# Two DMA issues of the first attention moved: batch 0's value loads and the first store of maxima

## The chip, the cores and the metric

The kernel runs on one core of a Trainium2 chip. The metric is the time on the device, in microseconds. TensorE (PE), VectorE (DVE), ScalarE (ACT) and GpSimd (POOL) compute; SyncE (SP) only issues DMAs, and POOL issues some too. All DMAs of the core are carried by its 16 DMA engines.

## What is computed

Two transformer-like layers on x of shape 4 x 1024 x 128 in float32. The change lies in the first attention: 16 heads of width 8, a plain softmax over 1024 keys.

```python
def _L0_attn_ref(z, ln_scale, ln_bias, w_qkv, w_proj, b_proj):
    ...
    qkv = zn @ w_qkv
    ...
    scores = jnp.einsum('bhqd,bhkd->bhqk', q, k) / SCALING
    att = jax.nn.softmax(scores, axis=-1)
    out = jnp.einsum('bhal,bhlv->bhav', att, v)
    ...
    return z + out
x = L0_attn_z
xn = _layernorm(x, axis=-1)
s = _L0_attn_ref(xn, L0_attn_ln_scale, L0_attn_ln_bias, L0_attn_w_qkv, L0_attn_w_proj, L0_attn_b_proj)
g = _silu(_L0_ffn_ref(xn, ...))
x = x + s * g
```

The second layer (landmark attention and a mixture of experts) follows and isn't touched.

## The kernel before

The first attention is the function `layer0_attention`. Its unit is a pair of heads, `d`, of which there are 32 (`DUOS`); two pairs make a quad, whose operands lie in one of three slots (`SLOTS`). A quad's operands `b_q`, `b_k`, `b_qo`, `b_ko` and `b_v` come from DRAM with `load_quad`, which issues 13 DMAs on SP (four for each of three parts, and one for the values). Batch 0 is quads 0 to 3, pairs 0 to 7.

A pair is done in 8 groups `kb` of 128 keys (`TB` = 8). In each group PE makes four blocks of 512 scores (L724), ACT takes their exponential (L669), and PE multiplies the exponentials of the group before by the values (L700); `b_av` counts these finished groups over the whole stage, and so stands at 8 x d when pair d begins to be counted. Between groups PE makes the plain scores from which the row maxima of a pair further on are taken (L555, L556) and DVE reduces them (L611). In group 5 of pair d-1 PE transposes the maxima of pair d. DVE and POOL split the negated maxima into three bfloat16 parts `b_neg`, and SP stores them with three small DMAs into three more rows of that quad's `b_q` (`store_maxima`, L797 for each DMA). The matmuls L724 of pair d read these rows: PE waits for `b_m_loaded` before the first of them.

SP's order is written by hand: loads of quads 1 and 2, the maxima of pair 0, and then for each pair d the maxima of pair d+1, the numerators and sums of pair d (`store_values`, L804, four DMAs), in some pairs a piece of zeroing, and a part of a later quad (eight DMAs in odd steps, five in even ones). In the step d = 13 it is the eight.

Batch 0 is finished inside this stage (`EARLY` = 1). POOL loads its softmax sums, DVE inverts them, POOL stores the reciprocals, and in its step d = 14 POOL loads the numerators and the reciprocals (`load_values`, L761 into `d_num` and L763 into `d_den`, 512 KB each). DVE multiplies the two only at the end of pair 15 (L636), and PE projects the result in the last pair. POOL's step d begins with the maxima of pair d, that is in group 5 of pair d-1.

The prologue of the stage, before pair 0 can begin, is the maxima of pairs 0 and part of 1: PE and DVE alternate there, while quads 1 and 2 are being loaded.

Of the kernel before, what the change touches and what calls it, by code (L numbers as in the profile page):

```python
# [15 lines left out]
TB = T // P  # L16
# [148 lines left out]
SLOTS = 3  # L165
# [5 lines left out]
T_GROUP = 5  # L171
LEAD = ITEMS + LATE - 2 * T_GROUP
EARLY = 1
RECS = B - 1
PROJECT_AT = (0, 1, 2, 3)
E_RING = 12
# [346 lines left out]
def wait_for_parts(g, sp, b):  # L523

    for i in range(NPART):
        sp.wait_ge(g.sem(f"a_stored{i}"), STORED[i] * (b + 1))
    sp.wait_ge(g.sem("a_v_stored"), 16 * (b + 1))


def load_quad(g, sp, quad, c, parts=range(NPART + 1)):  # L530

    def moved(dst, src):
        sp.dma_start(dst, src).then_inc(g.sem(f"b_loaded{c}"), 16)

    for m in parts:
        if m == NPART:
            moved(g.v0[c][:, 0:HQ * P], g.v_ops[quad, :, :, :].rearrange("p h n -> p (h n)"))
            continue
        lo = NPART * HD * ((m + 2) % NPART)
        n = min(NPART * HD, MROWS - lo) // HD  # L540
        flat = "h i d t -> (i d) h t"
        moved(g.q0[c][lo:lo + NPART * HD, :, :], g.q_ops[quad, :, :, :, :].rearrange(flat))
        moved(g.k0[c][lo:lo + NPART * HD, :, :], g.k_ops[quad, :, m:m + NPART, :, :].rearrange(flat))
        odd = slice(MROWS + lo, MROWS + lo + n * HD)
        moved(g.qo[c][odd, :, :], g.q_ops[quad, 1:HQ:2, 0:n, :, :].rearrange(flat))
        moved(g.ko[c][odd, :, :], g.k_ops[quad, 1:HQ:2, m:m + n, :, :].rearrange(flat))
# [23 lines left out]
def layer0_attention(g):  # L570
# [6 lines left out]
    nc, sem = g.nc, g.sem  # L577
    with ExitStack() as mem:
# [6 lines left out]
        zeros = sb("b_zeros", [P, 2048])  # L585
        dens = sb("d_dens", [P, RECS, P])
        num = sb("d_num", [P, T])
        den = sb("d_den", [P, T])
        oT = sb("d_oT", [P, EARLY, T])
        sm = sb("d_small", [P, 5, TB])  # L590
# [11 lines left out]
    with nc.Block() as block:  # L602

        @block.vector
        def _(dve):
# [21 lines left out]
            for d in range(DUOS):  # L627
                for n in range(upto(d, -1), upto(d, TB - 1)):
                    item(n)
                b = d // 8 - 1  # L630
                if 0 <= b < RECS and d % 8 == 3:
                    dve.wait_ge(sem("d_dens"), 16 * (b + 1))
                    nc.vector.reciprocal(dens[:, b, :], dens[:, b, :]).then_inc(sem("d_recs"), 1)
                if 0 <= b < EARLY and d % 8 == 7:
                    dve.wait_ge(sem("d_loaded"), 32 * (b + 1))
                    nc.vector.tensor_tensor(oT[:, b, :], num[:, :], den[:, :], ALU.mult).then_inc(sem("d_oT"), 1)  # L636
            link = Link(dve, sem("d_step"))
            for b in range(EARLY):
                mine = slice(b * TB, (b + 1) * TB)
# [93 lines left out]
        @block.gpsimd  # L733
        def _(pool):
            nc.gpsimd.memset(zeros[:, :], 0.0).then_inc(sem("b_zeros"), 1)

            def parts(d):
                pool.wait_ge(sem("b_max_done"), seq.index((d, None)) + 1)
                nc.gpsimd.tensor_copy(neg[:, 1, :], neg_rest[:, :]).then_inc(sem("b_second"), 1)  # L739
                pool.wait_ge(sem("b_second"), d + 1)  # L740
                nc.gpsimd.tensor_tensor(neg[:, 2, :], neg_rest[:, :], neg[:, 1, :], ALU.subtract)\
                      .then_inc(sem("b_third"), 1)

            def load_sums(b):
                for s in range(2):
                    pool.wait_ge(sem(f"b_stored{s}"), 16 * 4 * 4 * (b + 1))
                src = g.av_out[b * 4:b * 4 + 4, :, HD, :].rearrange("q h (c t) -> (q h) c t", t=P)
                pool.dma_start(dens[:, b, :], src).then_inc(sem("d_dens"), 16)

            def store_reciprocals(b):  # L750
                pool.wait_ge(sem("d_recs"), b + 1)
                pool.dma_start(g.recs[b, :, :].rearrange("h (c t) -> h c t", t=P), dens[:, b, :])\
                  .then_inc(sem("d_recs_kept"), 16)

            def load_values(b):
                pool.wait_ge(sem("d_recs_kept"), 16 * (b + 1))
                if b < EARLY:
                    if b:
                        pool.wait_ge(sem("d_oT"), b)
                    src = g.av_out[b * 4:b * 4 + 4, :, 0:HD, :].rearrange("q h d t -> (q h) d t")  # L760
                    pool.dma_start(num[:, :], src).then_inc(sem("d_loaded"), 16)  # L761
                    src = g.recs[b:b + 1, :, :].rearrange("a h t -> (a h) t").unsqueeze(1).broadcast_to([H, HD, T])
                    pool.dma_start(den[:, :], src).then_inc(sem("d_loaded"), 16)  # L763

            def biased(b):

                xn = g.XN[:, b * TB:(b + 1) * TB, :]
                nc.gpsimd.tensor_tensor(xn, xn, g.bproj[:, :].unsqueeze(1).broadcast_to([P, TB, D]), ALU.add)\
                      .then_inc(sem("d_biased"), 1)

            for d in range(DUOS):
                parts(d)
                if 1 <= d <= B:
                    biased(d - 1)
                b = d // 8 - 1
                if 0 <= b < RECS and d % 8 == 3:
                    load_sums(b)
                if 0 <= b < RECS and d % 8 == 5:
                    store_reciprocals(b)
                if 0 <= b < RECS and d % 8 == 6:  # L780
                    load_values(b)
            for b in range(EARLY):
                pool.wait_ge(sem("d_var"), b + 1)
                nc.gpsimd.tensor_tensor(rstd8, v8, g.eps_pow[:, :], ALU.pow).then_inc(sem("d_rstd"), 1)

        @block.sync
        def _(sp):
            def store_maxima(d):


                for i in range(NPART):
                    if i == 0:
                        sp.wait_ge(sem("b_max_done"), seq.index((d, None)) + 1)
                    else:
                        sp.wait_ge(sem(("b_second", "b_third")[i - 1]), d + 1)
                    dst = q[d // 2 % SLOTS][ROWS + i:ROWS + i + 1, 2 * (d % 2):2 * (d % 2) + 2, :]
                    sp.dma_start(dst.rearrange("r h (t x) -> r (h t) x", x=P), neg[:, i, :])\  # L797
                      .then_inc(sem("b_m_loaded"), 16)

            def store_values(d):  # L800
                sp.wait_ge(sem("b_acc"), d + 1)
                for i in range(4):
                    dst = g.av_out[d // 2, 2 * (d % 2) + i // 2, :, i % 2 * BANK:(i % 2 + 1) * BANK]
                    sp.dma_start(dst, acc[32 * i:32 * i + 2 * HD, d % 2, :]).then_inc(sem(f"b_stored{d % 2}"), 16)  # L804

            disp = g.x_disp[0:E * CAP, :].rearrange("(q r) d -> q (r d)", q=E * 5)
            kept = g.y_tok[0:ENTRIES, :].rearrange("(q r) d -> q (r d)", q=P)

            def zero(piece):
                i = 2048 * piece  # L810
                if piece < DISP_PIECES:
                    n = min(2048, DISP_ROW - i)
                    sp.dma_start(disp[:, i:i + n], zeros[0:E * 5, 0:n]).then_inc(sem("disp_zeroed"), 16)
                else:
                    i -= 2048 * DISP_PIECES
                    sp.dma_start(kept[:, i:i + 2048], zeros[:, :]).then_inc(sem("disp_zeroed"), 16)

            for c in range(1, SLOTS):
                load_quad(g, sp, c, c)
            store_maxima(0)  # L820
            sp.wait_ge(sem("b_zeros"), 1)
            for d in range(DUOS):
                if d + 1 < DUOS:
                    store_maxima(d + 1)
                store_values(d)
                if d in ZERO_AT:
                    zero(ZERO_AT.index(d))
                new = (d - 1) // 2 + SLOTS
                if d and new < QUADS:
                    if d % 2:  # L830
                        sp.wait_ge(sem("b_av"), TB * (d + 1))
                        wait_for_parts(g, sp, new // 4)
                    load_quad(g, sp, new, new % SLOTS, (LATER, SOONER)[d % 2])
            for s in range(2):
                sp.wait_ge(sem(f"b_stored{s}"), 16 * 4 * QUADS)
            sp.wait_ge(sem("disp_zeroed"), 16 * PIECES)
# [12 lines left out]
def layer0_outputs(g):  # L849
# [60 lines left out]
    with nc.Block() as block:  # L910

        @block.vector
        def _(dve):
# [34 lines left out]
            def norm(n, part):  # L948

                done = n - EARLY + 1  # L950
                if part == 0:
# [274 lines left out]
        def _(sp):  # L1226
# [6 lines left out]
            load(EARLY)  # L1233
            src = g.av_out[RECS * 4:B * 4, :, HD, :].rearrange("q h (c t) -> (q h) c t", t=P)
            sp.dma_start(dens[:, :], src).then_inc(sem("c_dens"), 16)
# [762 lines left out]
```

## Time and profile before

| | |
|---|---|
| time, median of 3 runs | 1373.0 us |
| lowest and highest | 1372.49 and 1374.38 us |
| time of the profiled execution | 1378.67 us |
| its span in the profile | 1376.6 us |
| PE busy | 1248.7 us, 91% of the span |
| ACT busy | 852.0 us, 62% |
| DVE busy | 1008.9 us, 73% |
| first attention, pairs 0 to 31 | about 118.6 to 818 us |

A timeline row is: start, duration, engine, line, operation, out<-in, count, and in brackets the idle time of the engine just before it and what ended it. In the stage of the first attention PE is the engine that is nearly always busy, so its idle stretches, and those at a lower clock, are what the reader looks for.

### The profile page before, as it was taken

Reading aid. Unit: us, or ns where it says so; the run is one execution under the profiler, and the core shown is the slowest. Engines: PE = TensorE matmul, PEld = TensorE weight load, DVE = VectorE, ACT = ScalarE, POOL = GpSimd, SP = SyncE. Lnnn points to the kernel's source line nnn. Section 1 sums busy time; section 2 is a strip of 40 time slices with the busy share of each in tenths; the row PEclk is TensorE's granted clock in tenths of the full one; section 3 lists DMA queues with packets and bytes.
Section 4 is the critical chain, followed back from the end, with each engine's and each line's share of the span. In section 5 each row is a group of like instructions: output and inputs, shape, how many; then the busy total and the mean of one; then the engine's idle time right before and its main releaser. Section 6 shows DMA issues by size and latency. Waiting matters only on the chain. (4 is left out here: it accounts for less than half of the span.)

```text
span 1376.6 us, 25966 instructions
## 1 busy us (share of the span) xinstructions
PE 1248.7 (91%) x10305; PEld 578.2 (42%) x10305; DVE 1008.9 (73%) x1288; ACT 852.0 (62%) x1447; POOL 238.3 (17%) x309
## 2 busy tenths in 40 slices
PE   6967999999999999999999978988899799899990
PEld 4631222222221222222222225555599666678870
DVE  5878898998997988998999836664687488523324
ACT  3533888888886888888887875554412366533431
POOL 4200110000000000000000002000286122135560
PEclk9986999999998999999999999998999699999995
DMA  4763123232333223231321112100001111123316
GB/s 143 216 193 73 28 63 70 43 76 51 67 71 74 52 64 73 44 75 44 73 66 46 70 44 76 47 16 16 17 25 45 55 44 36 46 69 101 101 57 187
DMA packets 75205, 94.96 MB, mean 69 GB/s; under 512 B 13237, under 2 KB 44685, under 8 KB 74053
## 3 DMA queue, kind: packets, MB, share of 16 engines
q1 hardware_dynamic: 69996, 83.19, 23.4%
q0 software_dynamic: 5088, 10.12, 2.4%
q8 instruction: 81, 1.33, 0.4%
q14 instruction: 40, 0.32, 0.1%
HBM read 54.30 MB, written 38.56 MB: 67 GB/s over the span
## 5 line engine op out<-in xcount | busy, mean ns | idle before, releaser
L669 ACT ACTIVATE b_exp_ring<-psum 128x512 f32<-128x512 f32 x1024 | 555.5, 599 | 155.2 <-PE psum L724 152.0
L611 DVE TENSOR_REDUCE b_mx<-psum 128x2 f32<-128x1024 f32 x507 | 595.8, 1219 | 72.9 <-PE psum L556 71.8
L724 PE MATMUL psum<-b_q,b_k 75*128 75x512 bf16 x1024 | 313.5, 388 | 5.6 <-DMA b_q<-b_neg 4.1
L700 PE MATMUL psum<-b_exp_ring,b_v 128*32 128x512 f32 x2048 | 275.4, 609 | 0.9 <-ACT b_exp_ring L669 0.7
L724 PEld LDWEIGHTS psum<-b_q,b_k 75*128 75x128 bf16 x1024 | 79.4, 97 | 323.0 <-ACT b_exp_ring L669 221.2
L555 PE MATMUL psum<-b_k,b_q 64*128 64x512 bf16 x512 | 168.8, 395 | 25.7 <-DVE b_mx L611 10.6
L556 PE MATMUL psum<-b_ko,b_qo 64*128 64x512 bf16 x512 | 168.9, 395 | 0.0
L739 POOL CAST b_neg<-b_neg_rest 16x128 bf16<-16x128 f32 x32 | 9.0, 281 | 658.3 <-DVE b_neg_rest L622 658.3
L1831 ACT ACTIVATE e_hT<-psum,e_b 128x358 f32<-128x358 f32 (+3 forms) x96 | 53.7, 561 | 75.3 <-PE psum L1851 72.0
L555 PEld LDWEIGHTS psum<-b_k,b_q 64*128 64x128 bf16 x512 | 44.5, 93 | 128.4 <-issue 41.4
L700 PEld LDWEIGHTS psum<-b_exp_ring,b_v 128*32 128x32 f32 x2048 | 41.3, 108 | 109.1 <-issue 105.6
L1761 POOL DMA_INDIRECT y_tok<-e_y,e_dest x72 | 71.1, 987 | 70.5 <-DVE e_y L1803 51.3
L1271 POOL DMA_INDIRECT x_disp<-x_norm,row_sent x64 | 63.7, 996 | 89.6 <-PE psum L1629 79.6
L1861 PE MATMUL psum<-e_w,e_hT 128*128 128x128 f32 (+1 forms) x576 | 67.4, 277 | 0.0
L1861 PEld LDWEIGHTS psum<-e_w,e_hT 128*128 128x128 f32 (+1 forms) x576 | 64.6, 184 | 1.8
L1609 ACT ACTIVATE f_le<-f_lx 128x1024 f32<-128x1024 f32 x32 | 33.8, 1057 | 45.8 <-DVE f_lx L1571 45.8
L997 DVE TENSOR_REDUCE c_nm<-psum 128x1 f32<-128x1024 f32 x32 | 37.7, 1219 | 32.8 <-PE psum L1154 32.8
L1851 PE MATMUL psum<-e_xT,e_w 128*128 128x358 f32 (+3 forms) x192 | 60.2, 468 | 0.9 <-DVE e_xT L1775 0.9
L1101 ACT ACTIVATE c_en<-psum,c_nm 128x1024 f32<-128x1024 f32 x32 | 35.7, 1117 | 32.9 <-DVE c_nm L997 32.9
L1565 DVE TENSOR_REDUCE f_max<-psum 128x16 f32<-128x1024 f32 x32 | 39.2, 1225 | 22.7 <-PE psum L1629 21.9
L1179 PE MATMUL psum<-ident,c_en 128*128 128x128 f32 x256 | 36.7, 289 | 12.4 <-ACT c_en L1101 8.6
L1447 PE MATMUL psum<-i_x,i_az 64*64 64x64 f32 x1536 | 46.4, 218 | 1.5 <-DVE i_x L1378 1.5
(278 smaller groups left out, 1422.9 us busy)
## 6 DMA issues: line engine op xcount, KB each, us to landing
b_q<-q_ops SPq DMA_DIRECT2D x48, 192.0 KB
b_k<-k_ops SPq DMA_DIRECT2D x48, 192.0 KB
k_ops<-a_k SPq DMA_DIRECT2D x20, 256.0 KB, 3.5
x_disp<-b_zeros SPq DMA_DIRECT2D x13, 320.0 KB
e_x<-x_disp SPq DMA_DIRECT2D x8, 520.0 KB
v_ops<-a_vs SPq DMA_DIRECT2D x4, 1024.0 KB, 5.1
b_v<-v_ops SPq DMA_DIRECT2D x16, 256.0 KB
av_out<-b_acc SPq DMA_DIRECT2D x128, 32.0 KB, 1.7
```

The lines of the kernel that those rows point to most:

```text
L555: g.nc.tensor.matmul(g.bank(2 * (n % 2)), q[0:MROWS, 2 * p, t], k[0:MROWS, 2 * p, keys], start=True, stop=True)
L556: return g.nc.tensor.matmul(g.bank(2 * (n % 2) + 1), qo[MROWS:P, p, t], ko[MROWS:P, p, keys], start=True, stop=True)
L611: nc.vector.reduce_max(mx[:, d % 2, :, i // 2, i % 2], pair, AX.X).then_inc(sem("b_max_done"), 1)
L669: act.activation(ex[:, n % E_RING, :], g.bank(5 + n % 3), ACT.Exp, scale=ATT_SCALE)\
L700: last = nc.tensor.matmul(AV[32 * i:32 * i + 32, :], v[s][:, at_v:at_v + 32], ex[:, (4 * group + i) % E_RING, :], start=(kb == 0), stop=(k ...
L724: nc.tensor.matmul(g.bank(5 + n % 3), k[s][0:XROWS, h, kb * P:(kb + 1) * P], q[s][0:XROWS, h, half * BANK:(half + 1) * BANK], start=True, ...
L1271: pool.indirect_dma_start(g.x_disp[:, :], bass.IndirectOffsetOnAxis(g.rows_out[:, n:n + 1], 0), g.XNW[:, n % NT, :], None).then_inc(g.sem( ...
L1447: last = nc.tensor.matmul(out[half, i, :], lhs(n * GR + i, half), rhs(n * GR + i, half), start=True, stop=True)
L1761: pool.indirect_dma_start(g.y_tok[:, :], bass.IndirectOffsetOnAxis(dest[c][0:r, t:t + 1], 0), y[c][0:r, t, :], None).then_inc(sem(f"e_sent ...
L1831: act.activation(hT[c][:, i, lo:hi], g.ps[:, (3 + n % 3) * BANK:(3 + n % 3) * BANK + hi - lo], ACT.Gelu, bias=b1[c][:, i:i + 1]).then_inc( ...
L1851: nc.tensor.matmul(g.ps[:, (3 + n % 3) * BANK:(3 + n % 3) * BANK + hi - lo], w1[c][:, i * P:(i + 1) * P], xT[:, lo:hi], start=True, stop=T ...
L1861: last = nc.tensor.matmul(g.ps[0:r, col:col + D], hT[c][:, i, t * P:t * P + r], w2[c][:, i, :], start=(i == 0), stop=(i == HC - 1))
```

## The change

Two edits. POOL waits, before it issues the two value loads of batch 0, until `b_av` has reached 8 x 14 + 2 = 114, that is until two groups of pair 14 are done. And SP issues the three stores of pair 0's maxima between the load of quad 1 and that of quad 2, not behind both.

```diff
+VALUES_AT = 2
...
                 if b < EARLY:
                     if b:
                         pool.wait_ge(sem("d_oT"), b)
+                    pool.wait_ge(sem("b_av"), TB * (8 * (b + 1) + 6) + VALUES_AT)
                     src = g.av_out[b * 4:b * 4 + 4, :, 0:HD, :].rearrange("q h d t -> (q h) d t")
...
-            for c in range(1, SLOTS):
+            load_quad(g, sp, 1, 1)
+            store_maxima(0)
+            for c in range(2, SLOTS):
                 load_quad(g, sp, c, c)
-            store_maxima(0)
             sp.wait_ge(sem("b_zeros"), 1)
```

The order on SP at the beginning of the stage, before: the last loads of quad 2 (`b_q2` to `b_v2`), then pair 0's three stores of maxima into `b_q0`, then those of pair 1.

```order
L533 DMA b_q2<-q_ops 24x4x1024
L533 DMA b_k2<-k_ops 24x4x1024
L533 DMA b_qo2<-q_ops 24x2x1024
L533 DMA b_ko2<-k_ops 24x2x1024
L533 DMA b_v2<-v_ops 128x512
L797 DMA b_q0<-b_neg 1x16x128 [waits b_max_done]
L797 DMA b_q0<-b_neg 1x16x128 [waits b_second]
L797 DMA b_q0<-b_neg 1x16x128 [waits b_third]
L797 DMA b_q0<-b_neg 1x16x128 [waits b_max_done,b_zeros]
```

The same place after (line numbers are one or two higher): the end of quad 1's loads, the stores, and the beginning of quad 2's loads.

```order
L534 DMA b_ko1<-k_ops 24x2x1024
L534 DMA b_v1<-v_ops 128x512
L799 DMA b_q0<-b_neg 1x16x128 [waits b_max_done]
L799 DMA b_q0<-b_neg 1x16x128 [waits b_second]
L799 DMA b_q0<-b_neg 1x16x128 [waits b_third]
L534 DMA b_q2<-q_ops 24x4x1024
L534 DMA b_k2<-k_ops 24x4x1024
L534 DMA b_qo2<-q_ops 16x2x1024
```

The three stores have moved ahead of quad 2's 13 loads, and these now stand behind the waits for pair 0's maxima.

The order on POOL around pair 14, before: the maxima of pair 14, the two value loads, the maxima of pair 15.

```order
L752 DMA recs<-d_dens 128x128 [waits d_recs]
L739 CAST b_neg<-b_neg_rest 16x128 [waits b_max_done]
L741 TENSOR_TENSOR b_neg<-b_neg_rest,b_neg 16x128 [waits b_second]
L761 DMA d_num<-av_out 128x1x1024 [waits d_recs_kept]
L763 DMA d_den<-recs 128x1x1024
L739 CAST b_neg<-b_neg_rest 16x128 [waits b_max_done]
L741 TENSOR_TENSOR b_neg<-b_neg_rest,b_neg 16x128 [waits b_second]
```

And after:

```order
L753 DMA recs<-d_dens 128x128 [waits d_recs]
L740 CAST b_neg<-b_neg_rest 16x128 [waits b_max_done]
L742 TENSOR_TENSOR b_neg<-b_neg_rest,b_neg 16x128 [waits b_second]
L763 DMA d_num<-av_out 128x1x1024 [waits b_av,d_recs_kept]
L765 DMA d_den<-recs 128x1x1024
L740 CAST b_neg<-b_neg_rest 16x128 [waits b_max_done]
L742 TENSOR_TENSOR b_neg<-b_neg_rest,b_neg 16x128 [waits b_second]
```

Nothing has changed its place there; the first value load has one more wait, on `b_av`.

## Rows read from the trace of the kernel before

**Rows 1.** The page: span, and the group of PE's score matmuls (L724).

```profile
span 1376.6 us, 25966 instructions
...
L724 PE MATMUL psum<-b_q,b_k 75*128 75x512 bf16 x1024 | 313.5, 388 | 5.6 <-DMA b_q<-b_neg 4.1
```

**Rows 2.** Timeline of PE at the end of the prologue: start, duration, work, [idle before].

```profile
115.89 0.61 PE L556 MATMUL psum<-b_ko,b_qo 64*128 64x512 bf16 x1
118.61 1.90 PE L724 MATMUL psum<-b_q,b_k 75*128 75x512 bf16 x4 [2.11 <-DMA b_q<-b_neg]
```

**Rows 3.** Timeline of SP's queue: last load of quads 1 and 2, then three stores.

```profile
99.97 0.35 SPq L533 DMA_DIRECT2D b_v<-v_ops  x1
...
105.43 0.35 SPq L533 DMA_DIRECT2D b_v<-v_ops  x1
111.03 1.85 SPq L797 DMA_DIRECT2D b_q<-b_neg  x3
```

**Rows 4.** View of the tile b_neg, SP, 100 to 125 us: issue to landing.

```profile
DMA to landing us min/median/max: 6.3/6.3/6.6
```

**Rows 5.** Stretches: busy us (count) of PE, PEld, DVE, ACT, POOL; clock, DMA share, GB/s.

```profile
95.00:107.00 12.00, 6.39 (x24) 1.00 (x20) 11.52 (x11) 0.93 (x1) 1.45 (x1) 0.50 0.77 182
107.00:117.50 10.50, 5.08 (x17) 0.87 (x17) 10.22 (x12) 0.00 (x0) 0.70 (x2) 0.50 0.79 168
118.60:125.40 6.80, 6.79 (x22) 1.24 (x24) 2.36 (x2) 3.72 (x8) 0.00 (x0) 0.50 0.01 2
425.90:436.00 10.10, 10.09 (x34) 1.72 (x35) 3.42 (x4) 4.83 (x9) 0.00 (x0) 0.50 0.25 58
...
419.00:426.00 7.00, 5.01 (x33) 1.12 (x31) 6.13 (x6) 4.34 (x8) 1.11 (x3) 0.99 0.65 154
432.80:440.50 7.70, 7.70 (x43) 1.43 (x35) 4.62 (x4) 4.43 (x9) 0.00 (x0) 0.79 0.65 151
```

**Rows 6.** Timeline of PE: beginnings of pair 13 and of pair 14.

```profile
402.22 0.82 PE L724 MATMUL psum<-b_q,b_k 75*128 75x512 bf16 x3
402.97 1.07 PE L700 MATMUL psum<-b_exp_ring,b_v 128*32 128x512 f32 x8
...
425.91 1.46 PE L724 MATMUL psum<-b_q,b_k 75*128 75x512 bf16 x3 [1.99 <-DMA b_q<-b_neg]
...
430.68 1.46 PE L724 MATMUL psum<-b_q,b_k 75*128 75x512 bf16 x3
...
435.44 1.11 PE L724 MATMUL psum<-b_q,b_k 75*128 75x512 bf16 x3
```

**Rows 7.** Timeline of SP's queue, pairs 12 to 15.

```profile
396.63 1.78 SPq L797 DMA_DIRECT2D b_q<-b_neg  x3
405.50 1.71 SPq L804 DMA_DIRECT2D av_out<-b_acc  x4
...
418.26 1.77 SPq L797 DMA_DIRECT2D b_q<-b_neg  x3
430.92 1.71 SPq L804 DMA_DIRECT2D av_out<-b_acc  x4
432.80 0.31 SPq L533 DMA_DIRECT2D b_q<-q_ops  x1
...
446.49 1.78 SPq L797 DMA_DIRECT2D b_q<-b_neg  x3
```

**Rows 8.** Timeline of POOL: issue of the two value loads.

```profile
419.04 0.54 POOL L761 DMA_DIRECT2D d_num<-av_out  x1
419.57 0.54 POOL L763 DMA_DIRECT2D d_den<-recs  x1
```

**Rows 9.** View of the tile b_neg, SP, 416 to 424 us: issue to landing.

```profile
DMA to landing us min/median/max: 1.6/1.7/6.4
```

**Rows 10.** View of the tile d_num: its load, issue to landing.

```profile
DMA to landing us min/median/max: 5.2/5.2/5.2
```

**Rows 11.** View of the tile d_den: its load, issue to landing.

```profile
DMA to landing us min/median/max: 6.4/6.4/6.4
```

## The prediction

> **What bounds the kernel now.** I read the page first: in the first attention PE is busy all but continuously, so what counts is where PE stands still and where it runs at half clock. The group of the score matmuls L724 has one releaser worth asking about: 4.1 us of waiting for the DMA `b_q<-b_neg` [rows 1]. The waits view shows that these 4.1 us are two events, and the timelines find them: 2.11 us before pair 0 [rows 2] and 1.99 us before pair 14 [rows 6]. These are the two places that the change touches. In the first the stores are issued from 111.03 us and land 6.3 to 6.6 us after issue [rows 3, 4], while the median store in a quiet place takes 1.7 us [rows 9]. In the second the last of the three stores takes 6.4 us [rows 9]: it is issued at about 418.26 + 1.18 = 419.44 us, lands at 425.8, and PE starts at 425.91. POOL had issued 2 x 512 KB of value loads at 419.04 and 419.57 us [rows 8], which landed 5.2 and 6.4 us later [rows 10, 11], that is at 424.3 and 426.0. The third store came in together with them.
>
> The second event costs more than its wait. Behind it the granted clock is 0.50, the 1.2 GHz level, from 425.9 to 436 us, with PE busy throughout [rows 5]. Groups there begin 4.77 us apart (425.91, 430.68, 435.44) [rows 6]. The whole bill is read from the stores of successive pairs: 396.63 to 418.26 is 21.63 us, a normal pair; 418.26 to 446.49 is 28.23 us [rows 7]. So pair 14 costs 6.6 us too much: 2.0 of waiting and 4.6 of half clock.
>
> **The POOL edit (pair 14).** The two value loads keep their count, size and queue; they move from 419.04 us to the end of the second group of pair 14. Without the stall pair 14 would begin at 402.22 + 21.63 = 423.85 us. `b_av` reaches 114 with the value matmuls run during the third group: 2 x 2.7 us (21.63 / 8) on, plus 0.75 + 1.07 us [rows 6], so about 431.0 us. The stores for pair 14 then find the DMA engines empty, as in the other pairs, and land 1.7 us after issue, by 421.2, well ahead of 423.85. That takes away the 2.0 us and the fall of the clock behind them: 6.6 us of the profiled execution.
>
> What is late next? The moved loads meet the eight quad loads of SP's step 13. In pair 13 the stores of values are issued 3.3 us after the pair's first matmul (405.50 against 402.22), and in step 13 the quad loads begin 1.9 us behind them (430.92, 432.80) [rows 6, 7]; so from about 429.0 us. The DMA work of the values is 0.65 x 7.0 = 4.6 us of all engines, that of the eight loads 0.65 x 7.7 = 5.0 us [rows 5]; together 9.6. At the 0.79 share that a long backlog of quad loads reaches [rows 5] this takes 12.1 us, until 441.1. The stores of pair 15's maxima are issued from 418.26 + 21.63 = 439.9 to 441.1 us, behind the quad loads on the same queue; the third lands at about 441.1 + 1.7 = 442.8, and PE wants it at 423.85 + 21.63 = 445.5. Spare: 2.7 us. I take no new stall. On POOL the wait has only the maxima of pair 15 behind it, which are due 9 us later. DVE uses the values at the end of pair 15, some 30 us after they land. POOL's wait itself costs nothing for the same reason.
>
> Here a rule speaks against the mechanism. The rows say that a 4 KB store on SP's queue, issued 0.4 us after POOL's first load, landed with POOL's loads after 6.4 us [rows 8, 9]. The Trainium skill, DMA: Bandwidth & Descriptors, section "Queues, rings and completion order", says that a DMA engine takes turns between the queues that have work, a packet at a time. By that rule a small store should be held up by little more than a packet of the other queue; the third store would have been late for another reason, this edit would be worth nothing, and the sum would be the first wait alone. The trace does not agree with the quick turn, and I go by the trace.
>
> **The SP edit (start).** Quad 1's loads and the stores are now apart from quad 2's. DMA work from 95 to 117.5 us is 0.77 x 12 + 0.79 x 10.5 = 17.5 us for both quads [rows 5]; half of it, 8.8, is less than the 9.2 done by 107 us. So quad 1 is in by about 107, the stores are issued at 111.03 as before (that moment is set by DVE's maxima), nothing lies ahead of them, and the third, issued near 112.3, lands near 114.0. PE's last prologue matmul ends at 116.50 [rows 2]. The wait of 2.11 us goes, and what is late next is PE itself. PE then runs at the lower clock, as before: granted 0.50 until 125.4, 6.8 us after it resumed [rows 5]. If the clock rises 6.8 us after the new start, the gain is the 2.1 us. If it takes as long as behind the other stall, 10.1 us [rows 5], 3.3 us more are run at half clock, each costing 4.6 / 10.1 = 0.46 us: the gain is then 0.6. If it rises 3.3 us sooner, the gain is 3.6. I take 2.1, the row of this very place. Quad 2's 13 loads are issued behind the third store, from about 112.9 instead of 100.4 us, and with 8.8 us of work at 0.79 are in by some 125; pair 1's maxima are stored over 20 us after pair 0's, and quad 2 is read from pair 2 on. Nothing waits for them. Quad 1 is needed in pair 0 only.
>
> **Sum.** Against the profiled execution: 2.1 + 6.6 = 8.7 us, 1378.67 - 8.7 = 1370.0. The median is 5.7 us under that execution (1373.0). Nothing in the rows says of what these 5.7 us are made. If the timed runs have the same stalls and the profile merely adds to them, the sum gives 1373.0 - 8.7 = 1364.3. If the clock does not fall in them, because the same 2.0 us of idleness fall otherwise, then only the waits go: 1373.0 - 4.1 = 1368.9. The lowest and highest of the three runs are 1.9 us apart, which shows no run with and no run without a 4.6 us piece beside it; so both ends stand. The half clock lasted 10.1 us in one row and 6.8 in the other, so its price isn't fixed either. I take it at one half of 4.6, which gives 1373.0 - 2.1 - 2.0 - 2.3 = 1366.6.
>
> **Rivals.**
> *Only the first wait goes (0.14).* The moved values and the quad loads last longer together than I count; the third store for pair 15 is 2.7 + 2.0 us later than forecast and pair 15 begins with the stall that pair 14 had. For it: two queues at once, and a spare of only 2.7 us. Against: 9.6 us of work fit. Term of the POOL edit 0, time 1373.0 - 2.1 = 1370.9. The same time comes out if the reason for the late third store is not the values.
> *The start gains nothing (0.12).* The stores at 111 us are slow for a reason other than quad 2 ahead of them, or the clock rises later and eats the gain. Time 1366.6 + 2.1 = 1368.7, 0.6 to 2.1 of it open.
> *Slower (0.05).* The same collision in pair 15, larger: it begins to decide when the DMA backlog ends after 445.5 us instead of 441.1. The eight loads are 151 GB/s x 7.7 us = 1,160 KB [rows 5], the values 1,024 KB. If the two queues together moved these 2,184 KB at only 100 GB/s, it would take 21.8 us from 429.0, until 450.8; the third store lands 1.7 us later and PE has stood for 7.0 us. With 4.6 us of half clock behind it that is 11.6 us on top of the forecast, 1378.2. Against it: the slower of the two pieces alone moved at 151 GB/s.
> *The change does not do what it says (0.03).* `b_av` at 114 is reached later than POOL arrives, so the wait does hold; only an earlier finish of the stores' own path could hide the effect: 1373.
> The forecast has the rest, 0.66, with a range of its own from 1363.5 to 1369.7.
>
> **How the numbers follow.** The range runs from 1363.5 (both stalls with the whole clock piece, and the clock a little sooner at the start) to 1371.3, which takes in the first two rivals. About 0.2% (2.7 us) is what a measurement of this kernel can tell from no change; so faster is under 1370.3. The forecast gives nearly all of its 0.66 to faster, the second rival most of its 0.12; the first, and the last, go to no change, with a small part of the forecast. Faster 0.77, same 0.17, slower 0.06.
>
> **What would show it right or wrong.** In the profile after: no row of L724 waiting for `b_q<-b_neg` at either place; the first L724 near 116.5 us; the stores before pair 0 landing in about 1.7 us; pair 14 as long as its neighbours, 21.6 us, at granted clock 1.00; POOL's two issues some 7 us after pair 14's first matmul. It is wrong if pair 15 starts with an idle stretch, if the clock falls in pair 14 all the same, or if the low clock at the start ends much later than 7 us after PE resumes. A profile that loses 8.7 us while the median loses 4 would say that the clock's fall belonged to the profiled execution.

## The result and the profile after

| | before | after |
|---|---|---|
| median | 1372.85 us (20 runs) | 1370.44 us (20 runs) |
| lowest and highest | 1369.74 and 1376.24 us | 1367.46 and 1373.99 us |
| time of the profiled execution | 1378.67 us | 1373.99 us |
| its span | 1376.6 us | 1372.0 us |

The ratio is 0.9977, with a 95% interval of 0.9969 to 0.9985: 3.2 us faster, 2.1 to 4.3. The changed kernel ran a second time beside its two parts and gave 0.9967 (0.9951 to 0.9983), 4.5 us. The forecast was 6.4 us. So the change is a small gain, with the forecast's sign and half to 70% of its size. The median after lies just above the 1370.3 us under which the forecast spoke of faster; the interval over all the runs leaves out no change.

In the trace both waits are gone. The page's group of score matmuls, which had 4.1 us of waiting for the store of maxima [rows 1], now has only ACT as a releaser (busy, mean ns | idle before it, releaser):

```profile
L725 PE MATMUL psum<-b_q,b_k 75*128 75x512 bf16 x1024 | 312.4, 387 | 1.5 <-ACT b_exp_ring L670 1.5
```

The timeline of SP's queue after: quad 1's last load, the three stores, quad 2 behind them. This answers to [rows 3].

```profile
99.75 0.35 SPq L534 DMA_DIRECT2D b_v<-v_ops  x1
110.56 1.85 SPq L799 DMA_DIRECT2D b_q<-b_neg  x3
112.45 0.55 SPq L534 DMA_DIRECT2D b_q<-q_ops  x1
...
117.67 0.35 SPq L534 DMA_DIRECT2D b_v<-v_ops  x1
```

The view of the tile `b_neg` on SP, 100 to 125 us: the stores land in 1.7 us instead of 6.3 [rows 4].

```profile
DMA to landing us min/median/max: 1.7/1.7/1.7
```

PE's timeline shows pair 0 without an idle stretch ahead of it, which answers to [rows 2].

```profile
115.42 0.61 PE L557 MATMUL psum<-b_ko,b_qo 64*128 64x512 bf16 x1
115.96 1.91 PE L725 MATMUL psum<-b_q,b_k 75*128 75x512 bf16 x4
```

Pair 14 now takes 417.94 to 439.58, 21.64 us, where it had taken 28.23 [rows 7], and the granted clock is 1.00 all through it:

```profile
396.30 1.78 SPq L799 DMA_DIRECT2D b_q<-b_neg  x3
...
417.94 1.78 SPq L799 DMA_DIRECT2D b_q<-b_neg  x3
...
439.58 1.82 SPq L799 DMA_DIRECT2D b_q<-b_neg  x3
```

POOL issues the value loads at 431.22 and 431.74 us, 7.7 us after the pair's first matmul at 423.53, and they land 8.5 and 10.2 us later, beside the quad loads. The views of `d_num` and `d_den`:

```profile
DMA to landing us min/median/max: 8.5/8.5/8.5
```

```profile
DMA to landing us min/median/max: 10.2/10.2/10.2
```

They hurt nobody. The stores for pair 15 (view of `b_neg`, 436 to 446 us) were a little slower:

```profile
DMA to landing us min/median/max: 1.8/2.2/2.4
```

The slowest was the first of the three, issued at 439.6 us. The same view over narrower stretches gives the third, issued at 440.8 us, 1.8 us: it was in at 442.6, and PE started pair 15 at 445.17 without a wait.

The place that did not come out as hoped is the clock at the start. Stretches after (same columns as [rows 5]): PE is busy from 115.9 us, and the granted clock stays at 0.50, 1.2 GHz, until 127.8.

```profile
115.90:127.80 11.90, 11.90 (x42) 1.96 (x40) 6.44 (x6) 6.18 (x12) 0.00 (x0) 0.50 0.66 131
127.80:136.00 8.20, 8.16 (x51) 1.88 (x47) 7.58 (x9) 6.62 (x13) 0.00 (x0) 1.00 0.00 0
```

That is 11.9 us at half clock against 6.8 before. From the stores of pair 0 to those of pair 13 the profile before has 396.63 - 111.03 = 285.60 us, this one 396.30 - 110.56 = 285.74: in these two executions all of the 2.1 us that the SP edit took away came back as half clock (5.0 us more of it, 2.3 us at the prediction's price of 0.46 us each).

Against the profile before, this one is 1376.6 - 1372.0 = 4.6 us shorter, where the prediction's sum had 8.7 for the pair of profiles. Pair 14 gives the 6.6 us forecast, the start up to pair 13 nothing. The rest lies where no edit is: the first store of maxima comes 0.5 us sooner, and the time from the stores of pair 15's maxima to the end is 932.4 us instead of 930.1.

### The profile page after: what moved, and what is told of

Same layout as the page of the kernel before. It is cut to its first block and busy times, and to the rows that moved or that the text cites. A ratio compares the mean times of both kernels' runs of the same rounds, so it can differ in the third digit from the quotient of the medians.

```text
span 1372.0 us, 25967 instructions
## 1 busy us (share of the span) xinstructions
PE 1249.1 (91%) x10305; PEld 580.1 (42%) x10305; DVE 1009.4 (74%) x1288; ACT 851.8 (62%) x1447; POOL 237.5 (17%) x309
```

## The experiments

Four kernels were first timed on one chip together: each part alone, both, and one that tries to win back the clock.

**The POOL wait alone.**

```diff
+VALUES_AT = 2
...
+                    pool.wait_ge(sem("b_av"), TB * (8 * (b + 1) + 6) + VALUES_AT)
```

> Only the POOL wait; SP's order as before. Theory A (the fall of the clock behind the wait before pair 14 happens in nearly every run of the kernel before, and the SP edit gives nothing): 2 to 6 us faster in the median, by itself all of the 2.4 us of the change or more. Theory B (in the timed runs only the wait of 2.0 us stands, the clock rarely falls): 1.5 to 2.5 us faster. Theory C (the timed runs have no stall before pair 14 worth naming): within 1 us. In the profile of all three: pair 14 lasts 21.6 us, the wait of about 2.1 us before pair 0 is still there.

Ratio 0.9991 (0.9976 to 1.0007): 1.2 us faster, between 3.3 faster and 1.0 slower. In its profile pair 14 lasts 441.64 - 420.00 = 21.64 us. So the POOL edit does what was forecast at its place, but is worth clearly less than 6.6 us in the timed runs. The interval reaches into what each of the three theories expected, so it does not choose between them; all three expected this length of pair 14. The wait before pair 0 is there, and larger than in the profile before:

```profile
119.60 1.90 PE L725 MATMUL psum<-b_q,b_k 75*128 75x512 bf16 x4 [3.57 <-DMA b_q<-b_neg]
```

**The order on SP alone.**

```diff
-            for c in range(1, SLOTS):
+            load_quad(g, sp, 1, 1)
+            store_maxima(0)
+            for c in range(2, SLOTS):
                 load_quad(g, sp, c, c)
-            store_maxima(0)
```

> Only the order on SP; POOL's value loads as before. If the clock rises a fixed time after pair 0 starts: 2.1 us faster. If the end of the low clock is not tied to pair 0's start and the earlier start is run at half clock: 0 to 1 us faster. In the profile: pair 0 starts without a wait, some 2 us sooner; pair 14 still begins with a wait of about 2 us, and lasts 23 to 28 us depending on the clock.

Ratio 0.9971 (0.9950 to 0.9992): 4.0 us faster, 1.1 to 6.9. The interval holds the 2.1 us of the first expectation; that the earlier start is run at half clock, 0 to 1 us, lies just outside it. No wait before pair 0. The clock rose only at 130.3 us, 13 us after the pair's start at 117.30, so the time from the start to the rise is not fixed, as the first expectation would have it. Pair 14 shows the old wait, and a short fall of the clock behind it: the timeline of SP's queue has 24.74 us from 419.74 to 444.48, 1.55 of them the wait and 1.55 half clock. PE's timeline, its first matmuls of pair 14:

```profile
426.95 1.16 PE L724 MATMUL psum<-b_q,b_k 75*128 75x512 bf16 x3 [1.55 <-DMA b_q<-b_neg]
```

**Both again.**

> The changed kernel again, on the same chip as its two parts. Its gain should be the sum of the two parts' gains within 1 us, near 2.4 us; its profile should again have no wait for b_neg anywhere.

Ratio 0.9967 (0.9951 to 0.9983): 4.5 us faster, against 1.2 + 4.0 = 5.2 for the parts. They add up within the 1 us expected; the gain is more than the 2.4 us expected, which its interval (2.3 to 6.7) just holds. No wait for `b_neg`. Here the clock rose at 122.9 us, only 6.0 us after pair 0's start at 116.92:

```profile
116.90:122.90 6.00, 6.00 (x21) 1.00 (x19) 4.04 (x4) 3.64 (x7) 0.00 (x0) 0.50 0.85 165
```

and from the first stores (111.52) to pair 13's (394.66) it has 283.14 us, 2.6 less than the other profile of the same kernel. The clock accounts for it: 5.8 us less of half clock, at 0.46 us each, is 2.7 us.

**The kernel before, profiled twice more.** No edit.

> The kernel before, a second look. The wait before pair 14 should be 1.5 to 2.1 us again. If the fall of the clock behind it is a matter of where the wait falls, pair 14 may last anything from 23.5 us (no fall) over 24.7 us to 28.2 us.

The wait before pair 0 was 2.52 us, that before pair 14 1.88, and behind it the clock did not fall at all. PE's timeline and the stretch, to be held against [rows 5, 6]:

```profile
425.51 0.82 PE L724 MATMUL psum<-b_q,b_k 75*128 75x512 bf16 x3 [1.88 <-DMA b_q<-b_neg]
428.12 0.82 PE L724 MATMUL psum<-b_q,b_k 75*128 75x512 bf16 x3
```

```profile
423.00:432.00 9.00, 7.12 (x48) 1.83 (x47) 6.23 (x7) 6.12 (x12) 0.00 (x0) 1.00 0.25 59
```

> The kernel before, a third look. Waits of 2 to 3.6 us before pair 0 and of 1.9 to 2.0 us before pair 14; pair 14 between 23.6 and 28.2 us, the part above 23.6 being the fall of the clock.

The wait before pair 0 was 2.54 us. That before pair 14 was only 0.83, outside what was expected (pair 14 took 22.53 us, under the 23.6 named), with no fall of the clock behind it: the last store landed in 5.3 us this time instead of 6.3 to 6.4.

**More behind the store.** The kernel before with a third 512 KB load behind the two at the old place.

```diff
+                    src = g.av_out[b * 4:b * 4 + 4, :, 0:HD, :].rearrange("q h d t -> (q h) d t")
+                    pool.dma_start(oT[:, 0, :], src).then_inc(sem("d_more"), 16)
...
                     dve.wait_ge(sem("d_loaded"), 32 * (b + 1))
+                    dve.wait_ge(sem("d_more"), 16)
```

> The kernel before, with a third load of 512 KB (the numerators once more, into the tile that DVE overwrites later) behind the two value loads at their old place. If the last store of pair 14's maxima is held up by the value loads ahead of it on the shared DMA engines, up to the end of their work, its landing goes from 6.4 us to 8.5 to 9.5 us and the wait before pair 14 from 2.0 to 4 to 5 us. If the store was issued before the third load arrived and only what is ahead of it counts, it stays at 6.4 us and 2.0 us. If the values were not the reason, it stays too, and so does pair 14 at up to 28.2 us.

The second of the three: the last store landed after 6.3 us, the wait was 1.89. POOL issued the loads at 420.67, 421.19 and 421.71 us, and the last store was issued at about 421.07. 512 KB issued 0.6 us behind it did not matter. The landing and the wait are as in the kernel before, so this run does not show what delays the store, only that load number three does not add to it.

**Nothing ahead of the store.** The changed kernel, in which the values are loaded at the old time, but by SP, behind the stores; POOL's two loads and its wait are left out.

```diff
                 if d + 1 < DUOS:
                     store_maxima(d + 1)
+                if d + 1 == 14:
+                    sp.wait_ge(sem("d_recs_kept"), 16)
+                    src = g.av_out[0:4, :, 0:HD, :].rearrange("q h d t -> (q h) d t")
+                    sp.dma_start(num[:, :], src).then_inc(sem("d_loaded"), 16)
+                    src = g.recs[0:1, :, :].rearrange("a h t -> (a h) t").unsqueeze(1).broadcast_to([H, HD, T])
+                    sp.dma_start(den[:, :], src).then_inc(sem("d_loaded"), 16)
```

> The changed kernel's order on SP, no wait on POOL; the two value loads are issued by SP, directly behind the three stores of pair 14's maxima, so at the old time but behind the stores. If order of issue is what counts: the stores land in 1.7 us, no wait before pair 14, pair 14 lasts 21.6 us, and the time is that of the changed kernel within 1 us. If value loads in flight slow the stores even from behind: the last store takes 3 us or more.

SP's timeline: the loads come 1.8 us after the first store and 0.6 us after the last.

```profile
416.21 1.78 SPq L792 DMA_DIRECT2D b_q<-b_neg  x3
418.03 0.59 SPq L824 DMA_DIRECT2D d_num<-av_out  x1
418.66 0.60 SPq L826 DMA_DIRECT2D d_den<-recs  x1
```

All three stores landed in 1.6 to 1.7 us; no wait, pair 14 lasts 437.84 - 416.21 = 21.63 us, ratio 0.9963 (0.9945 to 0.9982). So the value loads need not be put off: it is enough that they are issued behind the stores. The run changes the queue of the loads as well as their place in the order; that a load of POOL's queue 0.6 us behind the store does no harm either is known from the third load above.

**One load ahead of it.** The changed kernel, with the numerators issued at the old place and only the reciprocals put off.

```diff
-                    pool.wait_ge(sem("b_av"), TB * (8 * (b + 1) + 6) + VALUES_AT)
                     src = g.av_out[b * 4:b * 4 + 4, :, 0:HD, :].rearrange("q h d t -> (q h) d t")
                     pool.dma_start(num[:, :], src).then_inc(sem("d_loaded"), 16)
+                    pool.wait_ge(sem("b_av"), TB * (8 * (b + 1) + 6) + VALUES_AT)
```

> The changed kernel, but the load of the numerators is issued at its old place, ahead of pair 14's last store of maxima, and only the load of the reciprocals waits for two groups of pair 14. In the kernel before the last store landed 1.3 to 1.7 us after the numerators and before or with the reciprocals. If it is served behind the one load that was issued before it, it lands about 1.5 us after the numerators, which alone take some 3.5 to 4 us: landing 4.5 to 5 us after issue, and a wait before pair 14 of 0 to 0.7 us. If both value loads are needed to hold it up: 1.7 us and no wait. If one load holds it up as long as two: 6.4 us and a wait of 2 us.

The view of `b_neg` on SP, 412 to 426 us, and that of `d_num`:

```profile
DMA to landing us min/median/max: 1.6/3.3/4.2
```

```profile
DMA to landing us min/median/max: 4.5/4.5/4.5
```

The load was issued at 416.36 and was in at 420.9; the last store was issued at about 415.58 + 1.19 = 416.8 and landed at 421.0, with it, not 1.5 us behind it. One load ahead costs the store 2.5 us; PE had no wait. That lies between the expected cases: later than the 1.7 us of a store that one load does not touch, a little sooner than the 4.5 to 5 of one served behind it. The 3.3 is the second store, issued at about 416.17, 0.2 us ahead of the load. In the kernel before the second store also went out 0.2 us ahead of the load, and landed in 1.7 us [rows 7, 8, 9]; why it was held up here is open, and this is one profile. With the second load issued 0.1 us behind the store in the kernel before [rows 7, 8] it cost 4.7. So what is issued at nearly the same moment still counts, while the third load, 0.6 us later, did not.

**Trying to win back the clock.** The changed kernel with extra matmuls behind each pair of maxima matmuls in the prologue, into the bank of the value products, which the first of these overwrites. Their results are not used.

```diff
             for n in range(FIRST, upto(0, -1)):
                 item(n)
+                for _ in range(2):
+                    nc.tensor.matmul(AV, q[0][0:MROWS, 0, 0:P], k[0][0:MROWS, 0, 0:BANK], start=True, stop=True)
```

> The changed kernel, and in the prologue two extra matmuls of 512 columns behind each pair of maxima matmuls, into a bank that nothing reads before the first value matmul overwrites it. If what eats the SP edit's gain is the half clock at the beginning of pair 0 (11.8 us in the changed kernel's profile, at 0.46 us lost per us, so 5.4 us), then the clock is at its full level when pair 0 starts and this is 3 to 5.5 us faster than the changed kernel. If the half clock there is hidden by something else, it is the same; if the extra matmuls hold up the maxima, slower by up to 2 us.

Ratio to the kernel before 1.0001 (0.9985 to 1.0017): all of the gain lost, and at 4.6 us over the changed kernel's median (1373.72 against 1369.10) outside all that was expected. The stretches show why. PE is busy all of the time and the clock does not move, not before 128.0 us, while the maxima are held up and pair 0 starts at 120.11 us (25.7 us after the prologue's first matmul, 21.6 in the changed kernel).

```profile
94.40:112.00 17.60, 17.57 (x56) 7.02 (x57) 16.34 (x16) 1.10 (x1) 1.61 (x1) 0.50 0.56 112
112.00:120.10 8.10, 8.10 (x26) 2.92 (x23) 7.02 (x7) 0.00 (x0) 0.69 (x2) 0.50 0.43 94
120.10:128.00 7.90, 7.90 (x26) 1.37 (x26) 3.49 (x4) 4.24 (x8) 0.00 (x0) 0.50 0.74 156
```

The profiled execution has this late start too, though it was the fastest of the twelve, 1370.75 us.

The same with one float32 matmul of 128 columns on all 128 rows, in place of the two:

```diff
+                nc.tensor.matmul(AV[:, 0:P], g.ident[:, :], g.XN[:, n, :], start=True, stop=True)
```

> The changed kernel with one extra matmul behind each pair of maxima matmuls in the prologue, this time float32 over all 128 rows and 128 columns, about 0.45 us at the lower clock, which fits into the 0.5 us that PE has idle between them. In the run with extra bfloat16 matmuls on 64 rows PE was busy throughout the prologue and the clock stayed at its lower level. If rows and data type matter for the clock, it rises in the prologue here, pair 0 starts at the full level and the run is 2 to 4 us faster than the changed kernel. If the clock does not rise before pair 0 whatever PE does there, it is the same or up to 1 us slower.

In the profiled execution the clock did rise in the prologue, and pair 0 began at 117.16 at the full level:

```profile
106.00:113.00 7.00, 7.00 (x24) 3.59 (x24) 6.64 (x9) 0.00 (x0) 0.70 (x2) 0.50 0.03 8
113.50:117.00 3.50, 2.90 (x16) 1.44 (x16) 3.50 (x4) 0.00 (x0) 0.00 (x0) 1.00 0.44 109
```

Of its 12 runs five took 1365.4 to 1368.4 us with a mean clock of 0.963 to 0.965, and seven 1370.5 to 1373.8 with 0.953 to 0.958. By their clock, the early rise would be in those five; only one of them was profiled. The ratio is 0.9963 (0.9942 to 0.9985), no different from the changed kernel's 0.9967, so neither the 2 to 4 us expected nor a loss shows. The extra matmul took 0.73 us at the low clock, from its start to the next pair's, not the 0.45 expected, and does not fit into PE's idle time: the pairs of maxima come 1.27 us apart at the low clock instead of 1.13, which would cost the executions without the early rise some 2 us; that is argued, not shown. Two variants were meant to say what in the extra work made the difference. Their edits are shown against this kernel.

> As the run with one extra float32 matmul behind each pair of maxima matmuls, but on 64 of the 128 rows. There the clock rose at 113.4 us, before pair 0. If float32 is what made the difference to the bfloat16 extras, it rises in the prologue here too; if the rows are, it stays at 0.50 until after pair 0 has begun, as with the bfloat16 extras on 64 rows.

```diff
-                nc.tensor.matmul(AV[:, 0:P], g.ident[:, :], g.XN[:, n, :], start=True, stop=True)
+                nc.tensor.matmul(AV[:, 0:P], g.ident[0:MROWS, :], g.XN[0:MROWS, n, :], start=True, stop=True)
```

The clock stayed at 0.50 until 123.4 us, 7.6 us into pair 0. There is one execution of it, 1366.09 us, so it has no ratio.

> The changed kernel with one extra float32 matmul of 80 columns on all rows behind each pair of maxima matmuls; with 128 columns the pairs of maxima came 1.27 us apart instead of 1.13 while the clock was low. With 80 the prologue isn't held up. If the clock still rises before pair 0 in some executions, 1 to 3 us faster than the changed kernel; if the smaller extra work is too little for it, the same as the changed kernel.

```diff
-                nc.tensor.matmul(AV[:, 0:P], g.ident[:, :], g.XN[:, n, :], start=True, stop=True)
+                nc.tensor.matmul(AV[:, 0:80], g.ident[:, :], g.XN[:, n, 0:80], start=True, stop=True)
```

There too, until 123.3 us, with PE busy 22.77 of 23.00 us in the prologue (94 to 117 us). The pairs of maxima came 1.19 us apart, so the prologue was still held up a little, against what was expected; ratio 0.9988 (0.9973 to 1.0003), a smaller gain than the changed kernel's, though the intervals overlap. As the kernel with 128 columns seems to have the early rise in some executions only, one profile of each variant doesn't tell rows, type and amount of work apart. That stays open. No kernel here beats the changed one beyond its interval; the one with the values on SP equals it without the wait.

## Why the prediction was right, and where its size was off

**Both places, both mechanisms.** The two waits were named from the rows, and both were gone in every profile of the kernels that had the edit for them. The store before pair 14 was late because of the value loads issued just ahead of it: with nothing ahead it lands in 1.7 us, with one load in 4.2, with two in 5.3 to 6.4. The store before pair 0 was late because of quad 2's loads: in the kernels that issue them ahead of it the stores land in 6.3 to 8.3 us, in those that don't, and have no extra matmuls, in 1.7. What was not forecast is the clock behind it: that the low clock would end much later than 7 us after PE resumes was one of the prediction's own signs of being wrong, and in the profile after it ended 11.8 us after.

**The rule weighed against the change.** The Trainium skill, DMA: Bandwidth & Descriptors, section "Queues, rings and completion order", has each DMA engine take turns between queues; by that the small store should have been let through and the POOL edit been worth nothing. Here it was not let through: 2.5 us later behind one 512 KB load of another queue. What the same page says under "Issuing engines are not separate DMA queues", that all DMAs run on the same engines, is what the runs agree with. Whether the store is held up in these engines or in the memory behind them, no run here shows.

**What is late next.** The forecast had the backlog of quad and value loads end at 441.1 us; the reciprocals landed at 431.74 + 10.2 = 441.9. It had the third store in at 442.8 us and 2.7 us to spare before pair 15; it was in at 442.6, with 445.17 - 442.6 = 2.6. The two rivals that lived on this collision did not happen.

**The term that was too large: the clock behind pair 14.** Five profiles have the value loads at the old place:

| profile | wait before pair 14, us | pair 14, us | over 21.6 and the wait: half clock, us |
|---|---|---|---|
| before | 1.99 | 28.23 | 4.6 |
| third load added | 1.89 | 25.10 | 1.6 |
| SP order alone | 1.55 | 24.74 | 1.5 |
| before, second profile | 1.88 | 23.58 | 0.1 |
| before, third profile | 0.83 | 22.53 | 0.1 |

The mean excess is 3.2 us: 1.6 of waiting and 1.6 of half clock, where the sum took 2.0 and 2.3. The profile before was the extreme one. The prediction had said that the fall might belong to that execution and had taken half of it; that was the right doubt and still a little too much.

**The SP edit's 2.1 us.** Here both parts of the estimate moved. The wait before pair 0 was larger than in the one profile: 2.11, 2.52, 2.54, 3.41 and 3.57 us, mean 2.8. But the stretch of half clock that follows was longer on average with the earlier start: five profiles without the edit have 6.0 to 8.5 us of it after pair 0 begins, mean 7.2; five with it and without extra matmuls (changed kernel, again, SP order alone, values on SP, numerators early) have 11.8, 6.0, 13.0, 8.3 and 8.1, mean 9.4. The two groups overlap, so that the earlier start made it longer is likely and not shown. By the price of the prediction, 0.46 us for each, the 2.2 us more take 1.0 back. From the first stores of maxima to those of pair 13 the five without have 285.6, 285.7, 285.9, 287.8 and 287.7 us, the five with 285.7, 283.1, 286.2, 284.1 and 283.9: a gain of 1.9 us, the difference of two means whose groups are each 2 to 3 us wide. That the term came out near the 2.1 us forecast is luck in part: the wait was 0.7 us larger than the row that it was taken from, and the half clock took about as much back.

**The sum.** 3.2 + 1.9 = 5.1 us by these profiles, 6.4 forecast, 3.2 (2.1 to 4.3) and 4.5 (2.3 to 6.7) timed. Why the timed gain is smaller isn't shown; profiles are few, and pair 14 alone has a spread of 5.7 us over five of them. How the timed gain divides between the parts isn't settled: 1.2 and 4.0 us have intervals that hold both 3.2 and 1.9. The median after, 1370.44, lies outside the forecast's own range, 1363.5 to 1369.7, and inside the full one, up to 1371.3, which had been drawn wide enough to take in the first two rivals. In time the result is nearest to the first of them, 1370.9, whose mechanism, a stall before pair 15, did not occur. So the mechanism forecast is borne out, and the number is inside the range only by the room left for rivals: the term that was too large is the half clock behind pair 14, 2.3 us in the sum and 1.6 in the mean of five profiles.

**The offset of 5.7 us** between the profiled execution and the median was no cost of profiling. In the eight sets of ten or more timed runs that hold a profiled execution, that one lay between 3.6 us above and 4.1 us below the median, and the kernel before ran up to 1383 us without a profile. Most of the 5.7 us is pair 14. The third profile of the kernel before took 1372.15 us, near the median, and is 6.5 us shorter in its span than the first; of these 28.23 - 22.53 = 5.7 us lie in pair 14, and 1.0 us behind the stores of pair 15's maxima. So, as the prediction had allowed, the larger part of the clock's fall belonged to that one execution. Other scatter lies where no edit is: from the stores of pair 15's maxima to the end the fourteen profiled executions took between 926.6 and 933.7 us. In the second layer the low clock lasts longer in some of them, as the stretches of the kernel before's second profile and of the changed kernel's second profile show (the clock is the third number from the end).

```profile
1062.00:1100.00 38.00, 31.41 (x395) 24.26 (x393) 18.39 (x29) 12.88 (x23) 7.24 (x11) 0.56 0.17 50
```

```profile
1062.00:1100.00 38.00, 30.54 (x322) 22.05 (x322) 22.77 (x34) 15.51 (x23) 9.00 (x13) 0.69 0.20 60
```

## What to carry to other kernels

A small DMA that an engine waits for should be issued ahead of any large one, on whatever queue, and by a clear margin: 0.6 us was enough here, 0.1 us was not. Putting the large one behind it was worth as much as putting it off. Of a stall on PE, read the wait and the half clock behind it as two terms: the first is there in nearly every execution, the second in some, and one profile gives it no size. A start that is moved forward into a stretch of low clock can be worth less than it moved: in one pair of profiles all of it came back as half clock.

## What the runs showed of the hardware

A 4 KB store that normally lands in 1.7 us took 4.2 us with one 512 KB load of another queue issued 0.4 us ahead of it, and 5.3 to 6.4 us with a second one 0.1 us behind; a third, 0.6 us behind, added nothing. PE was busy for 33.6 us on end, nearly all of it with bfloat16 matmuls, before the granted clock left 1.2 GHz; 25.7 us of that lay before pair 0. The Trainium skill, TensorE: Matmul & The Clock Gate, section "What's actually happening", says that activity releases the throttle; here PE was busy for those 33.6 us before it was released. And a wait of nearly the same length, 1.88 and 1.99 us, left the clock at 2.4 GHz in one execution and was followed by 10 us at 1.2 GHz in another. Two 512 KB loads issued beside eight quad loads landed after 7.9 to 8.5 and 9.8 to 10.2 us, where they take 5.0 to 5.4 and 6.2 to 6.6 us without them.
